# Layer 2 attention: odd score steps of the first round in spare PSUM banks, and the next layer's first work dealt anew over the last batch

## The chip, the core and the metric

The kernel runs on one core of a Trainium2 chip. It is one launch that computes a whole model of four layers, each an attention and a feed-forward block. The metric is the device time of one execution in microseconds. The engines are TensorE (PE, its weight loads PEld), VectorE (DVE), ScalarE (ACT), GpSimd (POOL) and SyncE (SP), which issues the DMAs. Each runs its own instructions in their order and waits on semaphores for the others.

## The reference, cut to what matters

The change lies in the attention of layer 2 and in the first steps of the local attention behind it. In the code, batches are `b` = 0 to 7, there are 256 queries and 512 keys, 16 heads of 64 elements, and everything is float32.

```python
def _L2_xattn_ref(x, context, mask, Wq, Wkv, Wout, b_out):
    q = x @ Wq.T                                   # x is layer-normed
    k, v = jnp.split(context @ Wkv.T, 2, axis=-1)
    ...                                            # to heads
    sim = jnp.einsum('bhid,bhjd->bhij', q, k) * SCALE
    sim = jnp.where(mask[:, None, None, :], sim, max_neg)
    attn = jax.nn.softmax(sim, axis=-1)
    out = jnp.einsum('bhij,bhjd->bhid', attn, v)
    return out.transpose(0, 2, 1, 3).reshape(B, Nq, HEADS * DIM_HEAD) @ Wout.T + b_out

# local attention (layer 2, feed-forward block), its first lines
h = shift_token(x)
q, k, v = jnp.split(h @ wqkv, 3, axis=-1)
q, k = l2norm(q) * qs, l2norm(k) * ksc
q, k = rotary_xpos(q, k)
```

## The kernel before, in words

`wide_attention` (L1645 to L2084) does the attention of layer 2. A batch is cut in two rounds of 8 steps (`s` = 0 to 7 and 8 to 15). A round takes 8 of the 16 heads, a step 32 queries of these heads. A step has two units (`w` = 0, 1) of 128x512 scores:

- PE, `scores` (L2019): 8 matmuls of 64x32 weights and 512 columns (two records each in the trace) into two PSUM banks, `s_ps0` and `s_ps1`. All steps use the same two banks, so a step waits until DVE has read both units of the step before (`max_ready`, L2025).
- DVE, `maxima` (L1812): one instruction per unit (L1820) adds the mask, negates, copies the scores to SBUF and takes the maximum.
- ACT, `exponentials` (L1942, L1949), then DVE, `turn_probs` (L1823, L1832): two 32x32-block transposes a step into `pT`.
- PE, `outputs` (L2034): the value products of a whole round (L2046) and the spread inverse sums (L2052) go into the four banks of `pv_ps`, a round late: in steps 3, 5 and 7 of the next round. In batch 0's first round there is no round before, and `pv_ps` lies idle. Behind the last round all 128 products come at once (L2069).

ACT copies half of `pv_ps` (`copy_inv`, L1959), DVE multiplies it into `o` (`normalise_outputs`, L1845) and, behind the last round, PE starts the next value products only then.

Every engine looks one step ahead: in step `s` PE issues the scores of `s + 1`, then the step's jobs. Jobs are projections (XT, Q, K, V, OUT) and, in the last batch, LOCAL 0 to 7: the shifted tokens (0), their transpose (1), queries and keys of two token tiles (2 to 5) and their values (6, 7). They are set by tables (L1664 to L1671), and each goes through one of two ring banks, in turn: PE fills it, ACT (for OUT: DVE) drains it. A fill waits for the drain two jobs earlier. The local work of DVE and POOL on these results is in `FirstLocal`: `copy_half` (L1605) and `tables` (L1594), `sum_squares` (L1608), `rotate` (L1615), `normalise` (L1627), `power` (L1589). Before, LOCAL 0 to 5 stand in steps 10 to 15 and LOCAL 6 and 7 behind the last value products. The block ends with the output of batch 7, its moments and scaling (L1915 to L1918); then all engines meet and the local attention starts.

Of the kernel before, what the change touches and what calls it, by code (L numbers as in the profile page):

```python
# [14 lines left out]
B = 8  # L15
# [3 lines left out]
TPB = S // P  # L19
# [5 lines left out]
BLK = 32  # L25
# [1619 lines left out]
def wide_attention(m):  # L1645
# [21 lines left out]
    next_batch = {7: [(XT, 0)], 9: [(K, 0), (K, 1)], 10: [(K, 2), (K, 3)], 12: [(Q, 0), (Q, 1)]}  # L1667
    last_batch = {13: [(OUT, 0)], 14: [(OUT, 1)]}
    end_values = {8: [(V, 2), (V, 3)], 9: [(V, 4), (V, 5)], 10: [(V, 6), (V, 7)]}
    for_local = {10: [0], 11: [1], 12: [2], 13: [3], 14: [4], 15: [5]}  # L1670
    blocks_of = {3: range(0, 5), 5: range(5, 10), 7: range(10, 16)}  # L1671

    def step_jobs(b, s):
# [8 lines left out]
        return jobs  # L1682
    before = [(XT, 0, 0), (Q, 0, 0), (Q, 0, 1)]
    steps = {(b, s): step_jobs(b, s) for b in range(B) for s in range(STEPS)}
    behind = [(LOCAL, B - 1, 6), (LOCAL, B - 1, 7), (OUT, B - 1, 0), (OUT, B - 1, 1)]
    jobs = before + [job for b in range(B) for s in range(STEPS) for job in steps[b, s]] + behind
    number = {job: n for n, job in enumerate(jobs)}

    with ExitStack() as ctx:
# [24 lines left out]
        s_ps = [psum(m, ctx, f"s_ps{n}_l2x", [P, KV]) for n in range(2)]  # L1714
        pv_ps = psum(m, ctx, "pv_ps_l2x", [P, NC, 512])

        bank = lambda job: ring[number[job] % RING]
        fills = lambda job: m.filled[number[job] % RING].sem
        drains = lambda job: m.drained[number[job] % RING].sem
# [12 lines left out]
        with nc.Block() as block:  # L1732
# [15 lines left out]
            @block.gpsimd  # L1748
            def _(pool):
                def power(t0, t1, n):  # L1750
                    pool.wait_ge(*m.var_eps.after(n))
                    pool.tensor_tensor(rs[:, t0:t1], ve[:, t0:t1], k["minus_half"][:, 0:t1 - t0], ALU.pow).then_inc(m.row_rstd.sem, 1)

                def add_bias(b):
                    pool.wait_ge(*m.normed.after(TPB * (b + 1)))
                    rows = x[:, TPB * b:TPB * (b + 1), :]
                    pool.tensor_tensor(rows, rows, bo[:].unsqueeze(1).to_broadcast([P, TPB, D]), ALU.add).then_inc(m.bias_added.sem, 1)

                def spread_inv(n):
                    pool.wait_ge(*m.sums_inverted.after(n + 1))  # L1760
                    if n >= ROUNDS:
                        pool.wait_ge(*m.pv_done.after(n - 1))
                    pool.tensor_tensor(spread[n % ROUNDS][:], inv[:].unsqueeze(2).to_broadcast([P, 2 * QB, BLK]),  # L1763
                                       k["eye32"].unsqueeze(1).to_broadcast([P, 2 * QB, BLK]), ALU.mult).then_inc(m.inv_spread.sem, 1)

                def out_power(b):
                    cols = slice(TPB * b, TPB * (b + 1))
                    pool.wait_ge(*m.out_eps.after(b + 1))
                    pool.tensor_tensor(out_rs[:, cols], out_ve[:, cols], k["minus_half"][:, 0:TPB], ALU.pow).then_inc(m.out_rstd.sem, 1)

                power(0, TPB, 1)
                power(TPB, NT, 2)
                pool.wait_ge(*m.bias_loaded.after(16))
                add_bias(0)
                add_bias(1)
                for n in range(LAST + 1):
                    if n >= 3 and n % 2 == 1:
                        out_power((n - 3) // 2)
                    if n == LAST:
                        local.power(pool, 0)  # L1780
                    spread_inv(n)
                    if n % 2 == 1 and n // 2 + 2 < B:
                        add_bias(n // 2 + 2)
                local.power(pool, 1)
                out_power(B - 1)

            @block.vector
            def _(dve):
# [23 lines left out]
                def maxima(b, s):  # L1812
                    if s == 0:
                        dve.wait_ge(*m.mask_ready.after(b + 1))
                    for w in range(2):
                        n = 2 * s + w
                        dve.wait_ge(*m.scores_ready.after(UNITS * b + n + 1))
                        if UNITS * b + n >= 4:
                            dve.wait_ge(*m.turned.after(UNITS * b + n - 3))
                        dve.tensor_tensor_reduce(out=probs[n % 4][:], in0=s_ps[w][:], in1=mask_b[b % 2][:], scale=-1.0, scalar=3e38,  # L1820
                                                 op0=ALU.add, op1=ALU.min, accum_out=nmax[:, b % 2, n:n + 1]).then_inc(m.max_ready.sem, 1)

                def turn_probs(b, s):  # L1823
# [57 lines left out]
                for b in range(B):  # L1881
                    for s in range(STEPS):
                        n = ROUNDS * b + s // QB
                        if ahead(b, s)[0] < B:
                            maxima(*ahead(b, s))
                        turn_probs(b, s)
                        if s % QB == 1 and n >= 2:
                            normalise_outputs(n - 2)
                        if s % QB == 0 and n >= 1:
                            invert_sums(n - 1)  # L1890
                        for job in steps[b, s]:
                            drain(job)
                        if s == 14 and b > 0:
                            out_moments(b - 1)
                        if s == 15 and b > 0:
                            out_scale(b - 1)
                        if s == 6 and b + 1 < B:
                            convert_mask(b + 1)
                        if s == 10 and b + 2 < B:
                            scale(b + 2)  # L1900
                        if b + 1 == B and s == 9:
                            dve.wait_ge(*m.out_normed.after(2 * TPB))
                            local.copy_half(dve)
                            local.tables(dve)
                        if b + 1 == B and s == 14:
                            local.sum_squares(dve, 0)
                normalise_outputs(LAST - 1)
                invert_sums(LAST)
                dve.wait_ge(*m.scores_ready.after(UNITS * B))
                local.rotate(dve, 0, empty_local)  # L1910
                local.sum_squares(dve, 1)
                local.rotate(dve, 1, empty_local)
                local.normalise(dve, 0)
                normalise_outputs(LAST)
                local.normalise(dve, 1)  # L1915
                for job in behind:
                    drain(job)
                out_moments(B - 1)  # L1918
# [3 lines left out]
            def _(act):  # L1922
# [48 lines left out]
                        if s % QB == 0 and n >= 2:  # L1971
                            copy_inv(n - 2)
                copy_inv(LAST - 1)
                for job in behind[0:TPB]:
                    drain(job)
                copy_inv(LAST)

            @block.tensor
            def _(pe):
# [39 lines left out]
                def scores(b, s):  # L2019
                    r, qb = divmod(s, QB)  # L2020
                    if qb == 0:
                        for of in of_scores(b, r):
                            pe.wait_ge(*empty(of))
                    if (b, s) > (0, 0):
                        pe.wait_ge(*m.max_ready.after(UNITS * b + 2 * s))  # L2025
                    for w in range(2):
                        rows = slice(hd * w, hd * (w + 1))
                        for c in range(NC):
                            g = NC * r + c
                            ins = pe.matmul(s_ps[w][BLK * c:BLK * (c + 1), :], q[rows, g, BLK * qb:BLK * (qb + 1)], kT[rows, g, :],  # L2030
                                            start=True, stop=True)
                        ins.then_inc(m.scores_ready.sem, 1)

# [1559 lines left out]
```

## Time and profile before

| what | us |
|---|---|
| median of 3 runs (1711.23, 1711.42, 1713.07) | 1711.42 |
| the profiled execution's own time | 1709.85 |
| its span, first to last instruction | 1707.8 |
| `wide_attention`, from its first DVE statistics to its last scaling | 476.75 to 959.64 |
| PE, DVE, ACT, POOL busy, of the span | 1494.0, 1300.6, 1029.0, 569.3 |

Times in rows are microseconds from the span's start. A busy PE is one with a matmul in flight; PEclk 1.00 is TensorE's higher clock level (2.4 GHz), 0.50 the lower (1.2 GHz). The two ends of `wide_attention` are where the change is: 484 to 514 is batch 0's first round and the steps behind it, 908 to 960 the end of batch 7.

### The profile page before, as it was taken

The numbers are of one execution on the slowest core, as the hardware profiler recorded it, in microseconds if no ns is written. First come the engines' busy times: TensorE is split into PE (matmuls) and PEld (weight loads), VectorE is DVE, ScalarE is ACT, GpSimd is POOL, SyncE is SP. The second block draws the span as 40 slices with busy tenths as digits, with TensorE's granted clock in tenths as the row PEclk, the third lists the DMA queues.
The fourth block names the chain that finished last, engine by engine and source line by source line (L and its number), as shares of the span: only waits on it lengthen the run. The fifth ranks groups of instructions, "written<-read, shape, count | busy, mean of one in ns | idle before, by whom it ended". The sixth has DMA issues, their size and how long they took to land. (4 is left out here: it accounts for less than half of the span.)

```text
span 1707.8 us, 45809 instructions
## 1 busy us (share of the span) xinstructions
PE 1494.0 (87%) x17532; PEld 805.7 (47%) x17532; DVE 1300.6 (76%) x3513; ACT 1029.0 (60%) x2227; POOL 569.3 (33%) x618
## 2 busy tenths in 40 slices
PE   5886999997658999999998799987899787999976
PEld 3631344343423555555555566654566552333333
DVE  5636688885968787878877799857899557898848
ACT  2230666665936566666665499843898532777764
POOL 0306565621010000000001599615899104243200
PEclk9885899998869999999999999998999985999997
DMA  5123443411010000000000000010100003222100
GB/s 172 31 35 103 113 82 89 80 33 44 9 40 2 3 9 9 9 9 3 29 2 3 7 1 0 1 49 8 42 0 0 15 6 81 50 48 44 31 2 25
DMA packets 61570, 56.41 MB, mean 33 GB/s; under 512 B 9866, under 2 KB 53054, under 8 KB 61254
## 3 DMA queue, kind: packets, MB, share of 16 engines
q1 hardware_dynamic: 60518, 53.42, 13.0%
q8 instruction: 129, 2.11, 0.5%
q14 instruction: 59, 0.48, 0.1%
q10 hardware_dynamic: 864, 0.39, 0.1%
HBM read 30.59 MB, written 1.05 MB: 19 GB/s over the span
## 5 line engine op out<-in xcount | busy, mean ns | idle before, releaser
L1949 ACT ACTIVATE probs_l2x<-probs_l2x,nmax_l2x 128x512 f32<-128x512 f32 x256 | 182.8, 715 | 161.0 <-DVE nmax_l2x L1820 160.9
L1820 DVE CUSTOM_DVE_ANT_0 probs_l2x<-s_ps_l2x,mask_b_l2x 128x512 f32<-128x512 f32 x256 | 166.3, 687 | 92.3 <-PE s_ps_l2x L2030 90.8
L1087 DVE CUSTOM_DVE_ANT_0 junk_l1x<-s_ps_l1x,mask_b_l1x 128x512 bf16<-128x512 f32 x256 | 166.2, 686 | 44.6 <-PE s_ps_l1x L1292 42.7
L1090 DVE TENSOR_REDUCE nmax_l3x<-s_ps_l3x 128x1 f32<-128x512 f32 x256 | 163.7, 683 | 32.3 <-PE s_ps_l3x L1292 30.5
L1149 ACT ACTIVATE pT_l1x<-st_ps_l1x 128x1024 f32<-128x1024 f32 x128 | 131.0, 1023 | 72.6 <-PE st_ps_l1x L1277 72.5
L1832 DVE STREAM_TRANSPOSE pT_l2x<-probs_l2x 128x512 f32<-128x512 f32 x256 | 166.3, 688 | 0.0
L2030 PE MATMUL s_ps_l2x<-kT_l2x_first,q_l2x 64*32 64x512 f32 x2048 | 144.7, 622 | 16.8 <-DVE nmax_l2x L1820 15.9
L2046 PE MATMUL pv_ps_l2x<-pT_l2x,v_l2x_first 32*64 32x256 f32 x4096 | 122.3, 379 | 2.5 <-issue 2.5
L2641 POOL TENSOR_TENSOR rn_l2a_first<-ssc_l2a_first,consts 128x16 f32<-128x16 f32 x28 | 109.1, 3896 | 20.2 <-DVE ssc_l2a_first L2668 20.0
L2811 ACT ACTIVATE probs_l2a<-minus_s_l2a,nmax_l2a 128x128 f32<-128x128 f32 (+1 forms) x256 | 106.1, 424 | 9.5 <-DVE nmax_l2a L2716 9.5
L2046 PEld LDWEIGHTS pv_ps_l2x<-pT_l2x,v_l2x_first 32*64 32x64 f32 x4096 | 90.0, 131 | 39.2 <-issue 15.3
L1763 POOL TENSOR_TENSOR spread_l2x<-inv_l2x,consts 128x512 f32<-128x512 f32 x16 | 17.6, 1100 | 270.1 <-DVE inv_l2x L1839 270.1
L2597 POOL TENSOR_TENSOR v_l2x_first<-kT_l2x_first,tb_l2a_first 128x256 f32<-128x256 f32 x112 | 103.9, 958 | 3.3 <-ACT kT_l2x_first L2779 2.7
L2716 DVE CUSTOM_DVE_ANT_0 minus_s_l2a<-s_ps_l2a,consts 128x128 f32<-128x128 f32 (+1 forms) x256 | 67.3, 317 | 30.5 <-PE s_ps_l2a L2929 26.3
L1292 PE MATMUL s_ps_l3x<-kT_l3x_first,q_l3x 51*128 51x512 bf16 x192 | 74.3, 428 | 15.2 <-DVE nmax_l3x L1090 8.4
L1304 PE MATMUL pv_ps_l1x<-pT_l1x,v_l1x 128*32 128x256 f32 x1024 | 82.5, 396 | 1.6 <-ACT o_l1x L1157 1.4
L1292 PE MATMUL s_ps_l1x<-kT_l1x_first,q_l1x 48*128 48x512 bf16 x192 | 72.3, 433 | 12.1 <-DMA q_l1x<-parts_l1x_first 8.0
L1149 ACT ACTIVATE v_l2x_first<-st_ps_l3x 128x1024 f32<-128x1024 f32 x64 | 65.2, 1024 | 23.8 <-PE st_ps_l3x L1277 23.8
L1149 ACT ACTIVATE kT_l2x_first<-st_ps_l3x 128x1024 f32<-128x1024 f32 x64 | 65.2, 1023 | 20.4 <-PE st_ps_l3x L1277 19.9
L1277 PE MATMUL st_ps_l3x<-q_l3x,kT_l3x_first 54*128 54x256 bf16 x384 | 64.7, 280 | 0.0
L1277 PE MATMUL st_ps_l1x<-q_l1x,kT_l1x_first 51*128 51x256 bf16 x384 | 62.5, 283 | 0.0
L2030 PEld LDWEIGHTS s_ps_l2x<-kT_l2x_first,q_l2x 64*32 64x32 f32 x2048 | 23.6, 106 | 79.5 <-DVE nmax_l2x L1820 45.9
(533 smaller groups left out, 3637.9 us busy)
## 6 DMA issues: line engine op xcount, KB each, us to landing
mask_i_l1x<-in_mask SPq DMA_DIRECT2D x8, 512.0 KB, 4.8
maskT_i_l1x<-in_mask_t SPq DMA_DIRECT2D x8, 512.0 KB, 5.3
kT_l1x_first<-parts_l1x_first SPq DMA_DIRECT2D x60, 64.0 KB
kT_l3x_first<-parts_l3x_first SPq DMA_DIRECT2D x60, 64.0 KB
q_l1x<-parts_l1x_first SPq DMA_DIRECT2D x90, 32.0 KB
q_l3x<-parts_l3x_first SPq DMA_DIRECT2D x90, 32.0 KB
ctxT_l0x<-in_ctxT SPq DMA_DIRECT2D x9, 256.0 KB, 3.2
rows_l0x<-in_ctx SPq DMA_DIRECT2D x9, 256.0 KB, 4.4
```

The lines of the kernel that those rows point to most:

```text
L1087: dve.tensor_tensor_reduce(out=junk[w][:], in0=s_ps[w][:], in1=mask_b[b % 2][:, j, :], scale=-1.0, scalar=3e38, op0=ALU.add, op1=ALU.min, ...
L1090: dve.tensor_reduce(to, s_ps[w][:], AX.X, ALU.max, negate=True).then_inc(m.s_drained[w].sem, 1)
L1149: act.activation(pT[t % 4][:, :, 2 * j:2 * j + 2, :].rearrange("p w c t -> p w (c t)"), st_ps[j][:], ACT.Exp)\
L1277: ins = pe.matmul(st_ps[j][:, w, e * S:(e + 1) * S], kT[b % NST][rows, p, c * P:(c + 1) * P], q[b % NST][rows, p, :], start=not masked, st ...
L1292: pe.matmul(s_ps[w][:], q[b % NST][rows, p, j * P:(j + 1) * P], kT[b % NST][rows, p, :], start=True, stop=True)\
L1820: dve.tensor_tensor_reduce(out=probs[n % 4][:], in0=s_ps[w][:], in1=mask_b[b % 2][:], scale=-1.0, scalar=3e38, op0=ALU.add, op1=ALU.min, a ...
L1832: dve.transpose(pT[r][:, w, :, BLK * qb:BLK * (qb + 1)], probs[unit % 4][:].rearrange("p (k t) -> p k t", t=BLK))\
L1949: act.activation(probs[n % 4][:], probs[n % 4][:], ACT.Exp, bias=nmax[:, b % 2, n:n + 1], scale=-1.0, accum_out=sums[:, r, w, qb:qb + 1]). ...
L2030: ins = pe.matmul(s_ps[w][BLK * c:BLK * (c + 1), :], q[rows, g, BLK * qb:BLK * (qb + 1)], kT[rows, g, :], start=True, stop=True)
L2046: pe.matmul(pv_ps[hd * w:hd * (w + 1), c, 0:S], v[BLK * c:BLK * (c + 1), r, kb, hd * w:hd * (w + 1)], pT[r][BLK * c:BLK * (c + 1), w, kb, ...
L2641: pool.tensor_tensor(rn[:, cols], ssc[:, cols], k["minus_half"][:, 0:2 * NH], ALU.pow).then_inc(m.powers_ready.sem, 1)
L2811: act.activation(probs[n % (2 * DEEP)][:, cols], minus_s[n % (2 * DEEP)][:, cols], ACT.Exp, bias=nmax[:, u, TPB * n + j:TPB * n + j + 1], ...
```

## The change

Two parts.

**Scores.** In batch 0, steps 1, 3, 5 and 7 write their scores to banks 0 and 1 of `pv_ps` instead of `s_ps`, and DVE reads them there. The wait before a step's scores names the last step that used the same banks: two steps back in steps 2 to 8, none in step 1.

**Local work.** LOCAL 0 to 7 move to steps 5, 7, 11, 12, 12, 13, 15, 15 of the last batch; nothing but the output is left behind the value products. On DVE, `copy_half` and `tables` move from step 9 to step 4, `sum_squares(0)` from 14 to 13, `sum_squares(1)` and `rotate(0)` from behind the round to step 15 (ahead of `normalise_outputs(LAST - 1)`), and both `normalise` go ahead of `normalise_outputs(LAST)`. POOL does both powers before it spreads the last inverse sums.

```diff
-    for_local = {10: [0], 11: [1], 12: [2], 13: [3], 14: [4], 15: [5]}
+    for_local = {5: [0], 7: [1], 11: [2], 12: [3, 4], 13: [5], 15: [6, 7]}
...
-    behind = [(LOCAL, B - 1, 6), (LOCAL, B - 1, 7), (OUT, B - 1, 0), (OUT, B - 1, 1)]
+    behind = [(OUT, B - 1, 0), (OUT, B - 1, 1)]
...
+        spare = lambda b, s: b == 0 and s < QB and s % 2 == 1
+        score_bank = lambda b, s, w: pv_ps[:, w, :] if spare(b, s) else s_ps[w][:]
+        last_user = lambda b, s: s - 2 if b == 0 and 2 <= s <= QB else s - 1
...
                     if n == LAST:
                         local.power(pool, 0)
+                        local.power(pool, 1)
                     spread_inv(n)
...
-                local.power(pool, 1)
...
-                        if b + 1 == B and s == 9:
+                        if b + 1 == B and s == 4:
                             dve.wait_ge(*m.out_normed.after(2 * TPB))
                             local.copy_half(dve)
                             local.tables(dve)
-                        if b + 1 == B and s == 14:
+                        if b + 1 == B and s == 13:
                             local.sum_squares(dve, 0)
+                        if b + 1 == B and s == 15:
+                            local.sum_squares(dve, 1)
+                            dve.wait_ge(*m.scores_ready.after(UNITS * B))
+                            local.rotate(dve, 0, empty_local)
                 normalise_outputs(LAST - 1)
                 invert_sums(LAST)
-                dve.wait_ge(*m.scores_ready.after(UNITS * B))
-                local.rotate(dve, 0, empty_local)
-                local.sum_squares(dve, 1)
                 local.rotate(dve, 1, empty_local)
                 local.normalise(dve, 0)
+                local.normalise(dve, 1)
                 normalise_outputs(LAST)
-                local.normalise(dve, 1)
...
-                for job in behind[0:TPB]:
-                    drain(job)
...
-                    if (b, s) > (0, 0):
-                        pe.wait_ge(*m.max_ready.after(UNITS * b + 2 * s))
+                    if b > 0 or s > 1:
+                        pe.wait_ge(*m.max_ready.after(UNITS * b + 2 * (last_user(b, s) + 1)))
```

On PE the start of batch 0 reads as follows before, from the scores of step 0 on (`x7` stands for the other seven matmuls of a step):

```order
L2030 MATMUL s_ps_l2x<-kT_l2x_first,q_l2x 32x512 [waits bank0_drained,bank1_drained]
L2030 MATMUL s_ps_l2x<-kT_l2x_first,q_l2x 32x512 x7
L2030 MATMUL s_ps_l2x<-kT_l2x_first,q_l2x 32x512 [waits max_ready]
L2030 MATMUL s_ps_l2x<-kT_l2x_first,q_l2x 32x512 x7
L2030 MATMUL s_ps_l2x<-kT_l2x_first,q_l2x 32x512 [waits max_ready]
L2030 MATMUL s_ps_l2x<-kT_l2x_first,q_l2x 32x512 x7
```

and after the change:

```order
L2032 MATMUL s_ps_l2x<-kT_l2x_first,q_l2x 32x512 [waits bank0_drained,bank1_drained]
L2032 MATMUL s_ps_l2x<-kT_l2x_first,q_l2x 32x512 x7
L2032 MATMUL pv_ps_l2x<-kT_l2x_first,q_l2x 32x512 x8
L2032 MATMUL s_ps_l2x<-kT_l2x_first,q_l2x 32x512 [waits max_ready]
L2032 MATMUL s_ps_l2x<-kT_l2x_first,q_l2x 32x512 x7
L2032 MATMUL pv_ps_l2x<-kT_l2x_first,q_l2x 32x512 [waits max_ready]
L2032 MATMUL pv_ps_l2x<-kT_l2x_first,q_l2x 32x512 x7
```

Step 1 follows step 0 with no wait, and from step 2 on the wait named is for the maxima of two steps before.

On DVE the end of batch 7, from the last transposes on, reads before (`o_l2x<-pv_ps_l2x` is `normalise_outputs`; the rows on `kT_l2x_first`, `scratch_l2x` and `wq_l2x_first` are rotations and sums of squares):

```order
L1611 TENSOR_REDUCE ss_l2a_first<-scratch_l2x 128x16 [waits local_squared]
L1613 TENSOR_SCALAR ssc_l2a_first<-ss_l2a_first 128x16 [waits local_summed]
L1832 STREAM_TRANSPOSE pT_l2x<-probs_l2x 128x16x32 [waits probs_ready] x2
L1870 TENSOR_SCALAR y_l2a_first<-x_tok,out_mv_l2x,out_rs_l2x 128x128 [waits out_rstd]
L1870 TENSOR_SCALAR y_l2a_first<-x_tok,out_mv_l2x,out_rs_l2x 128x128
L1845 TENSOR_TENSOR o_l2x<-pv_ps_l2x,o_l2x 128x1024 [waits inv_copied]
L1839 RECIPROCAL inv_l2x<-sums_l2x 128x16 [waits inv_spread,probs_ready]
L1619 TENSOR_TENSOR kT_l2x_first<-kT_l2x_first,ta_l2a_first 128x1024 [waits bank0_drained,local_tables,scores_ready]
```

and after the change:

```order
L1835 STREAM_TRANSPOSE pT_l2x<-probs_l2x 128x16x32 [waits probs_ready] x2
L1873 TENSOR_SCALAR y_l2a_first<-x_tok,out_mv_l2x,out_rs_l2x 128x128 [waits out_rstd]
L1873 TENSOR_SCALAR y_l2a_first<-x_tok,out_mv_l2x,out_rs_l2x 128x128
L1611 TENSOR_REDUCE ss_l2a_first<-wq_l2x_first 128x16 [waits local_squared]
L1613 TENSOR_SCALAR ssc_l2a_first<-ss_l2a_first 128x16 [waits local_summed]
L1619 TENSOR_TENSOR kT_l2x_first<-kT_l2x_first,ta_l2a_first 128x1024 [waits bank1_drained,local_tables,scores_ready]
L1624 TENSOR_TENSOR scratch_l2x<-kT_l2x_first,tb_l2a_first 128x8x32 x4
L1848 TENSOR_TENSOR o_l2x<-pv_ps_l2x,o_l2x 128x1024 [waits inv_copied]
```

One pair of squares has left the place ahead of the transposes; the other pair and a rotation of five instructions now stand ahead of `normalise_outputs(LAST - 1)`.

## Rows read from the trace of the kernel before

**Rows 1.** Windows: engine, busy time, instructions; then PEclk, DMA share, GB/s.

```profile
484.00:514.00 30.00, 18.01 (x171) 4.31 (x170) 21.91 (x55) 15.23 (x40) 3.52 (x3) 0.72 0.00 2
514.00:930.00 416.00, 405.37 (x8119) 222.04 (x8112) 331.11 (x821) 263.83 (x639) 24.07 (x27) 1.00 0.03 8
```

**Rows 2.** Waits, 484 to 514: total us, times, longest.

```profile
PE s_ps_l2x L2030 <- DVE nmax_l2x L1820: 11.2, 8, 1.5
```

**Rows 3.** Timeline, steps 0 to 2 of batch 0: start, duration, engine, what.

```profile
484.81 1.09 PE L2030 MATMUL s_ps_l2x<-kT_l2x_first,q_l2x 64*32 64x512 f32 x16 [0.78 <-ACT q_l2x L1931]
...
487.27 0.60 DVE L1803 TENSOR_SCALAR xn_l2x<-x_tok,mv_l2x,rs_l2x 128x128 f32<-128x128 f32 x2
...
487.41 1.96 PE L2030 MATMUL s_ps_l2x<-kT_l2x_first,q_l2x 64*32 64x512 f32 x16 [1.50 <-DVE nmax_l2x L1820]
...
489.41 0.69 DVE L1820 CUSTOM_DVE_ANT_0 probs_l2x<-s_ps_l2x,mask_b_l2x 128x512 f32<-128x512 f32 x1 [1.53 <-PE s_ps_l2x L2030]
...
490.63 1.30 DVE L1832 STREAM_TRANSPOSE pT_l2x<-probs_l2x 128x512 f32<-128x512 f32 x2
...
492.77 0.69 DVE L1820 CUSTOM_DVE_ANT_0 probs_l2x<-s_ps_l2x,mask_b_l2x 128x512 f32<-128x512 f32 x1 [0.84 <-PE s_ps_l2x L2030]
```

**Rows 4.** Timeline, queries filled in step 4, maxima of steps 7 and 8.

```profile
502.76 2.73 PE L2009 MATMUL ring_l2x<-xnT_l2x,wq_l2x_first 128*128 128x256 f32 x8
...
509.05 0.69 DVE L1820 CUSTOM_DVE_ANT_0 probs_l2x<-s_ps_l2x,mask_b_l2x 128x512 f32<-128x512 f32 x1
...
511.80 0.68 DVE L1820 CUSTOM_DVE_ANT_0 probs_l2x<-s_ps_l2x,mask_b_l2x 128x512 f32<-128x512 f32 x1
```

**Rows 5.** Windows around PE's idle gaps, columns as in rows 1.

```profile
490.00:500.00 10.00, 5.89 (x48) 0.69 (x48) 7.48 (x19) 4.56 (x12) 0.00 (x0) 0.50 0.00 0
...
506.00:516.00 10.00, 4.50 (x74) 0.97 (x66) 9.45 (x24) 5.92 (x17) 0.00 (x0) 1.00 0.00 0
...
915.00:917.00 2.00, 2.00 (x20) 0.71 (x4) 0.84 (x3) 0.10 (x1) 0.00 (x0) 0.50 0.00 0
...
938.00:940.00 2.00, 1.08 (x40) 1.10 (x48) 2.00 (x4) 0.00 (x0) 0.95 (x1) 1.00 0.00 0
```

**Rows 6.** Timeline, PE in batch 7: LOCAL 0, next scores, next value products, LOCAL 6 and 7.

```profile
913.24 0.67 PE L1560 MATMUL ring_l2x<-y_l2a_first,consts 128*128 128x256 f32 x2 [2.44 <-ACT v_l2x_first L1935]
...
914.17 1.96 PE L2030 MATMUL s_ps_l2x<-kT_l2x_first,q_l2x 64*32 64x512 f32 x16
...
917.10 2.47 PE L2046 MATMUL pv_ps_l2x<-pT_l2x,v_l2x_first 32*64 32x256 f32 x80
...
946.45 1.98 PE L1572 MATMUL ring_l2x<-wqkv_l2a_first,hT_l2a_first 128*128 128x512 f32 x4
```

**Rows 7.** Timeline, last maxima to last output product.

```profile
929.34 0.69 DVE L1820 CUSTOM_DVE_ANT_0 probs_l2x<-s_ps_l2x,mask_b_l2x 128x512 f32<-128x512 f32 x1 [3.51 <-PE s_ps_l2x L2030]
...
935.76 0.57 DVE L1870 TENSOR_SCALAR y_l2a_first<-x_tok,out_mv_l2x,out_rs_l2x 128x128 f32<-128x128 f32 x2
...
937.59 1.23 DVE L1845 TENSOR_TENSOR o_l2x<-pv_ps_l2x,o_l2x 128x1024 f32<-128x1024 f32 x1 [1.26 <-ACT o_l2x L1959]
...
938.92 7.17 PE L2046 MATMUL pv_ps_l2x<-pT_l2x,v_l2x_first 32*64 32x256 f32 x256 [2.49 <-issue]
939.97 2.27 DVE L1624 TENSOR_TENSOR scratch_l2x<-kT_l2x_first,tb_l2a_first 128x256 f32<-128x256 f32 x4
942.16 1.21 DVE L1611 TENSOR_REDUCE ss_l2a_first<-wq_l2x_first 128x16 f32<-128x1024 f32 x1
...
943.65 3.81 POOL L1592 TENSOR_TENSOR rn_l2a_first<-ssc_l2a_first,consts 128x16 f32<-128x16 f32 x1 [2.70 <-DVE ssc_l2a_first L1613]
...
944.62 1.45 DVE L1624 TENSOR_TENSOR wq_l2x_first<-kT_l2x_first,tb_l2a_first 128x256 f32<-128x256 f32 x4
...
948.96 1.02 ACT L1959 ACTIVATE o_l2x<-pv_ps_l2x 128x1024 f32<-128x1024 f32 x1
...
951.29 5.47 PE L2016 MATMUL ring_l2x<-wo_l2x,o_l2x 128*128 128x128 f32 x32 [2.86 <-DVE o_l2x L1845]
```

More of the change, by code:

```diff
@@ L1819, in maxima @@
                             dve.wait_ge(*m.turned.after(UNITS * b + n - 3))
-                        dve.tensor_tensor_reduce(out=probs[n % 4][:], in0=s_ps[w][:], in1=mask_b[b % 2][:], scale=-1.0, scalar=3e38,
+                        dve.tensor_tensor_reduce(out=probs[n % 4][:], in0=score_bank(b, s, w), in1=mask_b[b % 2][:], scale=-1.0, scalar=3e38,
                                                  op0=ALU.add, op1=ALU.min, accum_out=nmax[:, b % 2, n:n + 1]).then_inc(m.max_ready.sem, 1)
@@ L2029, in scores @@
                             g = NC * r + c
-                            ins = pe.matmul(s_ps[w][BLK * c:BLK * (c + 1), :], q[rows, g, BLK * qb:BLK * (qb + 1)], kT[rows, g, :],
+                            ins = pe.matmul(score_bank(b, s, w)[BLK * c:BLK * (c + 1), :], q[rows, g, BLK * qb:BLK * (qb + 1)], kT[rows, g, :],
                                             start=True, stop=True)
```

## The prediction

> **What bounds the kernel now.** I read the windows first, to learn which engine fills each stretch. From 514 to 930 PE is busy 405 of 416 us at the full clock [rows 1]: there the order of PE's work sets the pace, and whatever is won ahead of this stretch is kept, as no fixed date lies in it. From 484 to 514 PE is busy only 18 of 30 us, at a mean clock of 0.72, and DVE 22 of 30 [rows 1]: nothing is full, so a chain bounds it. The list of waits names the chain: PE waits for maxima, eight times, 11.2 us [rows 2]. The timeline shows one turn of it: scores 1.96 us (487.41 to 489.37), two maxima (489.41 to about 490.7), and only then the next scores, because both steps use the same banks. The turn takes 492.77 - 489.41 = 3.36 us, of which DVE works 490.63 - 489.41 = 1.22 on maxima and 1.30 on transposes, 2.5 together [rows 3]. These scores run at the lower clock level (0.50 from 490 to 500 [rows 5]); at the higher one they take 1.09 [rows 3], and then the chain, 1.09 + 1.3 + gaps, is also 2.5: from step 7 on DVE stands with no idle time before it [rows 4]. So double banks can win only where the clock is low. Last I read the end of batch 7, where waits stand again: PE waits 2.44 us for a ring bank and then runs scores in 1.96 again [rows 6], and 2.49 before the last value products [rows 7].
>
> **First round, the scores.** Step 1's scores no longer wait; they follow step 0's (484.81 + 1.09) and are done by about 487, while DVE is busy until 487.27 + 0.60 = 487.87 [rows 3]. So the maxima of step 1 start at 487.87 instead of 489.41. From there DVE sets the turn, 2.5 us if scores come in time, and at half clock they do: 1.96 in a turn of 2.5. Step 7's maxima start at 487.87 + 6 x 2.5 = 502.9; before, 509.05 [rows 4]: 6.2 us earlier. One step can be late: behind step 5's scores stand two query fills, 2.73 us partly at half clock [rows 4]. Step 5's scores may start when step 3's maxima end (492.87 + 1.3 = 494.2), end at 496.2, the fills (2.7 to, at half clock throughout, 3.7) at 498.9 to 499.9, step 6's scores (1.1 to 2.0) at 500.0 to 501.9, and DVE wants them at 500.4: late by 0 to 1.5. I take 0.6, in the middle, since the denser PE work may raise the clock. The term is **-5.6** (bounds -4.7 and -6.2). PE writes one pair of banks while DVE reads the other, as it does now with value products beside maxima; I take 0.69 a maximum as it is.
>
> **Hand-off to the second round, a new gap.** Step 8's scores wait only for step 6 and are issued early; step 9's use the same banks as step 8's and wait for its maxima, at 511.80 - 5.6 + 1.3 = 507.5 [rows 4]. PE has finished step 8's scores and a transpose by about 503.5: idle some 4 us, where before no gap here was over 1.5 [rows 2]. This idle time costs nothing by itself, but the clock may fall: behind 2.44 us idle it was at 0.50 [rows 5, 6], behind 2.49 at 938 it stayed at 1.00 [rows 5, 7]. The low stretch after the former lasted from 913.24 to 917.10, 3.9 us [rows 6]. The same here costs at least nothing, where DVE covers it, and at most half of 3.9, 2.0, when the key fills (two of 128x512 in 1.98, by the same product in rows 6) make PE the bound. One turn of 3.36 for 2.5 is 0.9; I take **+1.0**.
>
> The Trainium skill, "TensorE: Matmul & The Clock Gate", section "Part 1: The HAM clock gate (the "warmup" mystery)", says that the throttled state is the default and activity releases it; its section "HAM oscillation" tells of a kernel which falls back at every long wait. By that rule alone both new gaps, this and the one at the end, would be followed by a low stretch, which is what my sum has; by the row at 938 one or both would not be.
>
> **Batch 7, up to its last scores.** LOCAL 0 leaves the place where it waited 2.44 us for ACT's drains [rows 6]; in step 5 only its own ring wait is left. But LOCAL 4 and 5 move ahead of the last scores, 1.98 us by the same two products [rows 6]. That is 0.4 won, less small ring waits where fills stand closer: 0 to 0.4, I take 0.1. With the gap goes the low stretch behind it: 3.9 us at half clock do 1.95 us of work, so 1.9 comes back, if no other gap over 2 us arises here, and I find none. Together **-2.0** (bounds 0 and -2.3). DVE's copy and tables in step 4 (seven instructions of at most 128x256, of which four take 1.45 [rows 7], so under 2.6) fall in its waits for scores, one of which was 3.51 [rows 7].
>
> **The end.** Call the start of the last maxima M (929.34 before [rows 7]). Before: y scaled by M + 7.0 (936.33), pv normalised from M + 8.25, last value products from M + 9.6, output products from M + 21.95. After: the first squares (1.21, with their small companion 1.3) have left, so y is scaled by M + 5.7. Then come the second squares, 1.3, and a rotation: 1.1 (943.5 to 944.62) and four smaller ones in 1.45 to 2.27, in all 2.6 to 3.4 [rows 7]. Normalising starts at M + 9.6 to 10.4 and takes 1.23; the last value products start at M + 10.9 to 11.7, **1.3 to 2.1 later**, and PE's gap of 2.49 grows to 3.8 to 4.6. They and the sums take 946.45 - 938.92 = 7.5 [rows 6, 7], to M + 18.4 to 19.2. Before, ACT's copy then came at 948.96, 2.5 after the products, because LOCAL 6 and 7 were filled and drained first [rows 6, 7]; now it follows at once. Copy 1.02, multiply 1.23 and hand-overs 0.2: output products at M + 20.9 to 21.7, 0.3 to 1.1 earlier; I take 0.7. What DVE does meanwhile (rotation 2.6, four of 128x1024 at 1.23 as in rows 7) is 7.5 us, ends with the products and is covered by the copy; if it were a microsecond longer it would show. POOL's second power (3.81) starts by M + 8, is wanted at about M + 15, and the spread of the inverse behind it at M + 18. Against this stands the clock: a gap of about 4 us, a low stretch of 3.9 within 7.5 us of matmuls, +1.9. The output products run at the low level already before (5.47 for 32), so nothing is added there. Together **+1.2** (bounds -1.1 and +1.6).
>
> **Sum.** -5.6 + 1.0 - 2.0 + 1.2 = -5.4. The profiled execution took 1709.85, so 1704.45. The three runs have a median of 1711.42, 1.57 more than that execution; the same difference taken, the forecast is 1711.42 - 5.4 = 1706.0. With all bounds good, -6.2 + 0 - 2.3 - 1.1 = -9.6 (1701.8); with all bad, -4.7 + 2.0 + 0 + 1.6 = -1.1 (1710.3).
>
> **Rivals.**
> - The clock stays high in both new gaps. For it: the gap at 936.4, and 44% busy PE at 1.00 between 506 and 516 [rows 5]. Against: both gaps are longer than the one that was followed by 0.50. -5.6 - 2.0 - 0.7 = -8.3: 1703.1.
> - The gain is mostly used up: step 6 late by the full 1.5, PE the bound in the whole low stretch of the hand-off, a low stretch again somewhere in batch 7 before its last scores, and rotation and clock both at their dear end: the sum above, -1.1, 1710.3. For it: each price has a row; against: they are independent, and the gap at 911 surely closes.
> - Slower: the low clock does not last 3.9 us behind the hand-off but runs on into the second round of batch 0. The 30 us from 484 show it can: 490 to 500 is all low, with PE 59% busy [rows 5]. Every microsecond of it in PE-bound steps costs 0.5, so it decides from 11 us more than I count; 16 more cost 8: 1711.4 - 5.4 + 8 = 1714. Against: there the chain kept PE idle every turn, while from step 9 on fills, scores and value products follow closely.
> - The banks free nothing, because something else held the scores. Rows 2 and 3 name only maxima; I give it no chance of its own.
>
> **How the numbers follow.** Forecast case 0.61, clock high in both 0.20, used up 0.13, low clock persisting 0.04, anything else 0.02. A measurement of this kernel tells 0.2%, 3.4 us, from no change, so 1708.0 is the border. The forecast and the high clock lie below it but for their dear edge (0.80 faster), used up lies within (0.15 with that edge), the rest is slower (0.05). The range 1702.4 to 1709.2 leaves out one in ten on either side.
>
> **What would show it.** In the profile after: maxima of step 1 at 487.9, turns of 2.5 until step 5, step 7 near 503.4; PE idle about 4 us before step 9's scores and a clock of 0.50 behind it; PE near 1.00 through batch 7 without the 2.44 gap; a gap of 3.8 to 4.6 before the last value products, the low clock in them, ACT's copy right behind. I am wrong if the turns stay over 3 us, if the first round's lead is gone before batch 1, or if the end from M to the last scaling (30.3 before) is longer than 32.5.

## The result, and the profile after

The changed kernel took 1700.35 us (median of 6 executions, 1697.82 to 1704.45) against 1711.43 for the kernel before (6, 1711.08 to 1713.70; three of them are those of the table above): ratio 0.9935, interval 0.992 to 0.995, or 11.1 us less. The forecast was 1706.0, the range 1702.4 to 1709.2. The direction was right, the gain was twice the forecast, and the time lies below the range.

The profiled execution took 1697.82 us, its span is 1695.8. Windows of the first round with the steps behind it, and of the rest up to the last maxima (columns as in [rows 1]):

```profile
479.00:509.00 30.00, 20.70 (x189) 6.08 (x190) 26.17 (x68) 17.67 (x47) 3.84 (x4) 0.73 0.00 1
509.00:919.00 410.00, 403.32 (x8091) 220.91 (x8091) 326.95 (x808) 262.77 (x634) 23.04 (x26) 1.00 0.03 8
```

Over the same 30 us from the first scores DVE now works 26.2 us where it worked 21.9 [rows 1]. The timeline (against [rows 3, 4]) of the first turns, of step 7's and 8's maxima, and of step 9's scores:

```profile
479.18 1.96 PE L2032 MATMUL s_ps_l2x<-kT_l2x_first,q_l2x 64*32 64x512 f32 x16 [0.78 <-ACT q_l2x L1935]
480.86 1.97 PE L2032 MATMUL pv_ps_l2x<-kT_l2x_first,q_l2x 64*32 64x512 f32 x16
...
485.47 0.65 DVE L1823 CUSTOM_DVE_ANT_0 probs_l2x<-s_ps_l2x,mask_b_l2x 128x512 f32<-128x512 f32 x1
...
487.89 0.65 DVE L1823 CUSTOM_DVE_ANT_0 probs_l2x<-pv_ps_l2x,mask_b_l2x 128x512 f32<-128x512 f32 x1
...
497.56 0.65 DVE L1823 CUSTOM_DVE_ANT_0 probs_l2x<-pv_ps_l2x,mask_b_l2x 128x512 f32<-128x512 f32 x1
...
500.29 0.68 DVE L1823 CUSTOM_DVE_ANT_0 probs_l2x<-s_ps_l2x,mask_b_l2x 128x512 f32<-128x512 f32 x1
...
501.64 1.96 PE L2032 MATMUL s_ps_l2x<-kT_l2x_first,q_l2x 64*32 64x512 f32 x16 [3.61 <-DVE nmax_l2x L1823]
...
506.90 3.50 PE L2013 MATMUL ring_l2x<-ctxT_l2x,wk_l2x_first 128*128 128x512 f32 x4
```

Step 1 follows step 0 at once, both at the lower clock (1.96 and 1.97 us); the turns are 487.89 - 485.47 = 2.42 us; step 7's first maxima start 497.56 - 479.18 = 18.4 us after the first scores, where it was 509.05 - 484.81 = 24.2 [rows 3, 4]. Then PE stands 3.61 us, and what follows runs at the lower clock: the scores of steps 9 and 10 in 1.96, the first two key fills in 3.50. In batch 7 the gap of 2.44 us [rows 6] is gone: LOCAL 0 has no idle time before it, and from 880 to 929, past the last scores, the clock stays at its higher level. LOCAL 0 in the timeline, and the window:

```profile
884.01 0.67 PE L1560 MATMUL ring_l2x<-y_l2a_first,consts 128*128 128x256 f32 x2
```

```profile
880.00:929.00 49.00, 45.62 (x964) 26.87 (x956) 39.05 (x97) 29.41 (x67) 7.23 (x4) 1.00 0.01 3
```

The end, against [rows 7] (the wait of 3.47 us is called "issue" by the profile, but DVE's multiplication, from 928.21, ends just before the products start):

```profile
918.96 0.69 DVE L1823 CUSTOM_DVE_ANT_0 probs_l2x<-s_ps_l2x,mask_b_l2x 128x512 f32<-128x512 f32 x1 [2.20 <-PE s_ps_l2x L2032]
...
923.87 0.56 DVE L1873 TENSOR_SCALAR y_l2a_first<-x_tok,out_mv_l2x,out_rs_l2x 128x128 f32<-128x128 f32 x2
...
925.70 1.23 DVE L1619 TENSOR_TENSOR kT_l2x_first<-kT_l2x_first,ta_l2a_first 128x1024 f32<-128x1024 f32 x1
926.84 1.44 DVE L1624 TENSOR_TENSOR scratch_l2x<-kT_l2x_first,tb_l2a_first 128x256 f32<-128x256 f32 x4
928.21 1.21 DVE L1848 TENSOR_TENSOR o_l2x<-pv_ps_l2x,o_l2x 128x1024 f32<-128x1024 f32 x1
...
929.52 8.85 PE L2048 MATMUL pv_ps_l2x<-pT_l2x,v_l2x_first 32*64 32x256 f32 x256 [3.47 <-issue]
...
938.90 1.02 ACT L1963 ACTIVATE o_l2x<-pv_ps_l2x 128x1024 f32<-128x1024 f32 x1 [11.72 <-PE pv_ps_l2x L2054]
...
941.24 3.84 PE L2018 MATMUL ring_l2x<-wo_l2x,o_l2x 128*128 128x128 f32 x32 [2.43 <-DVE o_l2x L1848]
```

The value products start 10.6 us after the last maxima (9.6 before) and take 8.85 instead of 7.17; the output products come 22.3 after them (21.95 before) but take 3.84 instead of 5.47.

Now each trace in four parts: ahead of the stage, its first batch, its middle and end, and what lies behind. "Stage" runs from the start of step 0's scores to the start of the last scaling; batch 1 is its first maxima. All times are in us. The first four rows are four profiled executions of the kernel before, the next three of the changed one; the rest are the experiments. PEclk is that of the first 200 us, in code that is the same in all of them.

| execution | PEclk 0 to 200 | start | to batch 1 | to last maxima | to last scaling | stage | behind |
|---|---|---|---|---|---|---|---|
| before, 1 | 0.81 | 484.81 | 50.19 | 394.33 | 29.97 | 474.5 | 748.5 |
| before, 2 (e5) | 0.85 | 478.06 | 50.20 | 394.42 | 29.97 | 474.6 | 750.2 |
| before, 3 (e10) | 0.81 | 485.69 | 50.12 | 394.48 | 29.92 | 474.5 | 750.4 |
| before, 4 (e11) | 0.85 | 479.55 | 53.48 | 392.92 | 31.66 | 478.1 | 752.3 |
| changed, 1 | 0.85 | 479.18 | 47.56 | 392.22 | 28.66 | 468.4 | 748.2 |
| changed, 2 (e6) | 0.85 | 480.56 | 46.60 | 392.23 | 28.66 | 467.5 | 748.9 |
| changed, 3 (e12) | 0.83 | 482.08 | 47.57 | 392.23 | 28.66 | 468.5 | 748.4 |
| e1 scores alone | 0.80 | 486.50 | 46.56 | 394.38 | 29.97 | 470.9 | 749.2 |
| e2 local alone | 0.85 | 481.89 | 50.22 | 392.18 | 28.65 | 471.1 | 749.1 |
| e3 power early | 0.86 | 476.50 | 50.21 | 394.41 | 32.71 | 477.3 | 752.1 |
| e4 power back | 0.85 | 479.16 | 47.55 | 392.18 | 28.63 | 468.4 | 749.4 |
| e7 step 9 too | 0.83 | 483.57 | 44.21 | 392.23 | 28.66 | 465.1 | 748.3 |
| e8 rotate behind | 0.84 | 482.02 | 47.89 | 392.24 | 26.00 | 466.1 | 750.3 |
| e9 both | 0.83 | 483.60 | 44.20 | 392.24 | 29.19 | 465.6 | 751.0 |

In the first pair of traces the stage is 6.0 us shorter, and 5.6 of the 12 us lie ahead of it, where nothing was changed. The experiments had to say why.

### The profile page after: what moved, and what is told of

The parts are those of the page before. It is cut to its first block and busy times, and to the rows that moved or that the text cites. A ratio compares the mean times of both kernels' runs of the same rounds, so it can differ in the third digit from the quotient of the medians.

```text
span 1695.8 us, 45799 instructions
## 1 busy us (share of the span) xinstructions
PE 1479.6 (87%) x17522; PEld 801.5 (47%) x17532; DVE 1301.7 (77%) x3513; ACT 1029.6 (61%) x2227; POOL 568.6 (34%) x618
## 5 line engine op out<-in xcount | busy, mean ns | idle before, releaser
L1823 DVE CUSTOM_DVE_ANT_0 probs_l2x<-s_ps_l2x,mask_b_l2x 128x512 f32<-128x512 f32 x248 | 161.1, 687 | 86.9 <-PE s_ps_l2x L2032 85.2
L2032 PE MATMUL s_ps_l2x<-kT_l2x_first,q_l2x 64*32 64x512 f32 x1984 | 137.7, 612 | 11.0 <-DVE nmax_l2x L1823 10.1
L2970 PE MATMUL t_ps_l2a<-consts,probs_l2a 128*128 128x128 f32 x384 | 56.6, 284 | 4.8 <-ACT probs_l2a L2813 4.4
```

The source lines that it names most:

```text
L1823: dve.tensor_tensor_reduce(out=probs[n % 4][:], in0=score_bank(b, s, w), in1=mask_b[b % 2][:], scale=-1.0, scalar=3e38, op0=ALU.add, op1=A ...
L2032: ins = pe.matmul(score_bank(b, s, w)[BLK * c:BLK * (c + 1), :], q[rows, g, BLK * qb:BLK * (qb + 1)], kT[rows, g, :], start=True, stop=True)
```

## The experiments

**e1 and e2: each part alone.** e1 has only `spare`, `score_bank` and `last_user`, e2 only the rest of the diff.

> The kernel before with the banks of the first round alone; the last batch as before. Inside wide_attention both theories expect the same: step 7's second maxima 5.9 us earlier after step 0's scores than before (24.24 us there), of which about 3.3 are given back at the hand-off, so 2.6 us ahead from batch 1 on. They differ in what lies ahead of it. Theory A (the part ahead of the stage, 5.7 us of the changed kernel's gain, is not made by the edit but by the phase in which TensorE's clock steps fall in unchanged code, and any change to the program can set it anew): the stage may start at 479 or at 485 us, and need not start where it does in the changed kernel: total 1703 or 1709. Theory B (the edit itself moves the early stages): a start at 479.2, total near 1703. Theory C (it is chance between executions): the start scatters from run to run and the median of the times is 1708.8, only the 2.6 below before.

> The kernel before with the local attention's first work dealt anew; all scores in the two old banks. Inside wide_attention: first round as before (24.24 us from step 0's scores to step 7's maxima), batch 7 up to the last maxima 2.05 us shorter, the end from the last maxima to the last scaling 29.0 instead of 30.3: together 3.4. Theory A (clock phase in unchanged code): start of the stage at 479 or 485 or elsewhere, total 1708.0 or 1702.3. Theory B (the edit): which of the two parts carries the 5.7 us must show, this one or the scores. Theory C (chance): median 1708.0.

e1: 1706.51 us (median of 12 executions; ratio to the kernel before 0.9975, interval 0.9961 to 0.9990). e2: 1707.57 (12; 0.9990, 0.9967 to 1.0013), not told from no change by its time. By the stage both do what was expected of them: e1 3.6 us to batch 1 (its first scores ran in 1.09 us and not in 1.96, which is the 0.9 over 2.6), e2 2.15 and 1.3. So the parts are independent within what the clock leaves open: 2.6 to 3.6 and 3.4 alone, 6.0 to 7.0 together. The starts, 486.50 and 481.89, are not that of the changed kernel: theory B has no part that carries the 5.7 us.

**e3 and e4: one POOL call moved**, in the kernel before (e3); e4 takes the same move back in the changed one.

```diff
                         local.power(pool, 0)
+                        local.power(pool, 1)
...
-                local.power(pool, 1)
```

> The kernel before with one POOL call moved: local.power(1) right behind local.power(0). The second squares come late here, so POOL's last spread waits for them; by the rows the power is wanted only at the very end, but the spread then starts about 4 us later than before, at M + 22, where the sums wait: inside the stage 0 to +3 us. Ahead of the stage nothing is touched at all. Theory A: the start of the stage moves off 484.8 (or off before's clock steps in the first 200 us) although nothing there is edited. Theories B and C: it stays at 484.8, within 0.5 us.

> The changed kernel with POOL's second power put back behind the spread of the last inverse sums. The power takes 3.1 us of the 6.2 ahead of the spread; spread and power are both done before the value products end, so inside the stage 0 (at most 0.5). Theory A: the start of the stage may leave 479.2 and the total may be anything from 1700 to 1706. Theories B and C: 1700.4, start at 479.2 (B) or scattered (C).

e3 took 1716.02 us (12), ratio 1.0033, interval 1.0015 to 1.0052: slower, by 2.6 to 8.9 us. Of this 2.7 us stand in the stage's end, as its trace shows; where the rest comes from, if it is more than scatter, no run shows.

```profile
934.58 3.81 POOL L1592 TENSOR_TENSOR rn_l2a_first<-ssc_l2a_first,consts 128x16 f32<-128x16 f32 x1 [5.19 <-DVE ssc_l2a_first L1613]
938.36 1.94 POOL L1763 TENSOR_TENSOR spread_l2x<-inv_l2x,consts 128x512 f32<-128x512 f32 x1
...
940.34 0.69 PE L2052 MATMUL pv_ps_l2x<-spread_l2x,consts 32*64 32x256 f32 x16 [2.49 <-POOL spread_l2x L1763]
```

The spread stands behind a power that waited 5.19 us for late squares, and PE waits 2.49 us for it; in the changed kernel, where the squares come in step 15, the same order costs nothing (e4: 1702.1, ratio 0.9953, interval 0.9934 to 0.9973; stage 468.4 as the changed one). And e3 starts the stage at 476.50, 8.3 us ahead of the first profile of before, with not one instruction changed ahead of it. That fells theory B, which had it at 484.8. (The expectation put theory C beside it there; as C was put for e1, a start that scatters, it allows 476.50.) Theory A, that any edit can set the early clock anew, is left by e3 and needs the next runs.

**e5, e10, e11: the kernel before again; e6, e12: the changed one again.** No edit.

> The changed kernel itself once more, beside many executions of the kernel before. Theory C (the stretches of low clock in unchanged code fall differently in every execution, whichever kernel): inside wide_attention the same as in the first profile to 0.1 us or so (step 7's maxima 18.38 after step 0's scores, batch 1 at 47.56, end 28.66 after the last maxima), while the start of the stage lies anywhere from 479 to 488 in prof time; the median over the executions then lies nearer to 1711 - 6 = 1704 than to 1700.35. Theory B (the edit moves the early stages): start at 479.2 again, median 1700.4.

> The kernel before once more, timed beside itself: the ratio must be 1.000, and the width of its interval says what such a comparison can tell. Theory C (the low clock ahead of wide_attention falls differently in each execution): the start of the stage leaves 484.8 by some us, either way, inside the stage all is as in the first profile (24.2 to step 7's maxima, 50.2 to batch 1, 394.3 to the last maxima, 30.0 to the end). Theory B (each kernel has its own fixed early stages): start at 484.8 within 0.5.

> As the last: another execution and another profile of the kernel before. Theory C: start between 476 and 487. What is open is whether the kernel before starts the stage late on the average (485) and the changed one early (479 to 480), which would explain a difference over 6 to 7 us, or both around 481.

> The kernel before, a fourth profile. The same question as in the last; theory C expects a scatter of the start of about 3 us (standard deviation) around 481, theory B 484.8.

> The changed kernel, a third profile, and a third comparison with the kernel before. Theory C: start anywhere between 476 and 487, inside the stage 46.6 to 47.6 to batch 1, 392.2, 28.7; ratio such that both medians differ by 6 to 7 us plus or minus 2. Theory B: start at 479 to 480 for the third time, median about 1701, ratio 0.9937.

The kernel before timed against itself (one set of 35 executions, against 12, 9 and 9 more) gave ratios of 0.9999, 1.0016 and 0.9996, with intervals about 0.0018 wide to either side: 3 us. The changed kernel gave 0.9937 (0.9924 to 0.9950) and 0.9958 (0.9942 to 0.9975). The starts of the kernel before, 484.81, 478.06, 485.69 and 479.55, scatter over 7.6 us with no edit at all, the last three on one chip. So theory C holds ahead of the stage, and no edit is needed to move the start, as theory A would have it. Whether an edit shifts the mean of the start by a microsecond or two, four and three profiles can't tell. In all fourteen profiles the start follows the clock of the first 200 us: 486.50 at 0.80, 484.81 and 485.69 at 0.81, 482 to 484 at 0.83 and 0.84, 478 to 482 at 0.85, 476.50 at 0.86. Going from 0.86 to 0.80 over 200 us is 24 us more at half clock, at most 12 us of work; 10.0 are seen. Between the first two profiles of the kernel before, the same instructions are 6.4 us apart by 185.5 us, of 6.75 at the start of the stage, and the distance grows where engines wait for matmuls. What makes the low stretches fall differently is not shown.

One forecast of theory C failed: for e6 it put the median nearer to 1704 than to 1700.35, and it was 1701.33 (6). In e12 the medians, 1703.10 and 1708.67, are 5.6 us apart, within its 6 to 7 plus or minus 2.

Theory C as I wrote it was also too simple inside the stage, which was to repeat to about 0.1 us. In e6 step 0's scores ran at the higher clock and batch 1 came 46.60 us after them, not 47.56. e11 is the kernel before and is 3.5 us longer there. PE at its hand-off and at its end:

```profile
507.40 1.96 PE L2030 MATMUL s_ps_l2x<-kT_l2x_first,q_l2x 64*32 64x512 f32 x16 [1.20 <-DVE nmax_l2x L1820]
510.77 1.96 PE L2030 MATMUL s_ps_l2x<-kT_l2x_first,q_l2x 64*32 64x512 f32 x16 [1.40 <-DVE nmax_l2x L1820]
512.66 3.78 PE L2011 MATMUL ring_l2x<-ctxT_l2x,wk_l2x_first 128*128 128x512 f32 x4
...
911.35 0.67 PE L1560 MATMUL ring_l2x<-y_l2a_first,consts 128*128 128x256 f32 x2 [2.44 <-ACT v_l2x_first L1935]
...
912.17 1.09 PE L2030 MATMUL s_ps_l2x<-kT_l2x_first,q_l2x 64*32 64x512 f32 x16
...
935.53 8.85 PE L2046 MATMUL pv_ps_l2x<-pT_l2x,v_l2x_first 32*64 32x256 f32 x256 [2.49 <-issue]
```

With gaps no longer than in the first profile the low clock stands behind the first round, where it did not; it is absent behind the 2.44 us gap, where it was [rows 6]; and it covers the last value products, 8.85 instead of 7.17 [rows 7]. Idle times of 2.4 to 3.2 us are followed by either level, and those of 3.45 to 3.61 us by the low one in every trace. The idle time ahead of seven pieces of PE work, and the level that the work behind it met, counted over the fourteen traces:

| work | idle time, us | low clock in it | high clock all through |
|---|---|---|---|
| output products, in the changed order | 2.43 | 1 (e9) | 7 |
| LOCAL 0 with the scores behind it, in the old order | 2.44 | 5 | 1 (e11) |
| last value products | 2.49 | 2 (e9, e11) | 6 |
| output products, in the old order | 2.86 | 6 | 0 |
| first products of the local attention, behind the stage | 3.20 to 3.21 | 2 (e3, e11) | 12 |
| last value products, in the changed order | 3.45 to 3.48 | 6 | 0 |
| scores of step 9 | 3.61 | 6 | 0 |

The first turns of e11 show one more thing. Its scores of steps 1 and 2 ran at the higher clock, on the two old banks:

```profile
482.15 1.09 PE L2030 MATMUL s_ps_l2x<-kT_l2x_first,q_l2x 64*32 64x512 f32 x16 [1.50 <-DVE nmax_l2x L1820]
...
483.28 0.69 DVE L1820 CUSTOM_DVE_ANT_0 probs_l2x<-s_ps_l2x,mask_b_l2x 128x512 f32<-128x512 f32 x1 [0.67 <-PE s_ps_l2x L2030]
...
485.77 0.69 DVE L1820 CUSTOM_DVE_ANT_0 probs_l2x<-s_ps_l2x,mask_b_l2x 128x512 f32<-128x512 f32 x1
```

The turn is 485.77 - 483.28 = 2.49 us, against 2.42 with double banks: at the higher clock the spare banks win next to nothing, and what they win depends on where the low clock falls.

**e7: step 9's scores in the spare banks too.**

```diff
-        spare = lambda b, s: b == 0 and s < QB and s % 2 == 1
+        spare = lambda b, s: b == 0 and s < QB + 2 and s % 2 == 1
-        last_user = lambda b, s: s - 2 if b == 0 and 2 <= s <= QB else s - 1
+        last_user = lambda b, s: s - 2 if b == 0 and 2 <= s <= QB + 2 else s - 1
```

> The changed kernel, with step 9's scores in the spare banks as well, so that they too wait only for maxima two steps back. Theory H1 (the 3.3 us given back behind the first round are the idle 3.6 us before step 9's scores and the low clock behind it): step 9's maxima at 23.5 after step 0's scores instead of 24.46, step 12's at 32.0 (31 to 33) instead of 35.2, batch 1 at 44.4 instead of 47.56; total 3.2 us under the changed kernel. Theory H2 (they are given back because PE is full from step 9 on, so nothing ahead of it is kept): step 12 at 35 and batch 1 at 47.5 as now, total unchanged.

The hand-off in its trace, PE:

```profile
500.96 1.09 PE L2032 MATMUL s_ps_l2x<-kT_l2x_first,q_l2x 64*32 64x512 f32 x16 [0.81 <-DVE nmax_l2x L1823]
501.99 0.44 PE L2007 MATMUL ring_l2x<-consts,xn_l2x 128*128 128x128 f32 x2
503.29 1.09 PE L2032 MATMUL pv_ps_l2x<-kT_l2x_first,q_l2x 64*32 64x512 f32 x16 [0.87 <-DVE nmax_l2x L1823]
506.04 1.09 PE L2032 MATMUL s_ps_l2x<-kT_l2x_first,q_l2x 64*32 64x512 f32 x16 [1.65 <-DVE nmax_l2x L1823]
507.06 1.98 PE L2013 MATMUL ring_l2x<-ctxT_l2x,wk_l2x_first 128*128 128x512 f32 x4
```

No gap over 1.93 us is left there (in e9, with the same edit, neither), scores take 1.09 and the fills 1.98. Step 9's maxima come 23.55 us after the first scores (24.46), step 12's 31.87 (35.21), batch 1 44.21: 3.3 us won, H1 by its numbers. PE was not full there (H2 falls): idle time and low clock gave the lead back. The total was to be 3.2 us under the changed kernel. It is 1702.05 (6; ratio 0.9938, interval 0.9918 to 0.9958), no lower than that of the changed kernel beside it, 1701.33; six executions that lie 12 us apart do not show 3.

**e8 and e9: the end.** e9 is e7 and e8 together.

```diff
-                            dve.wait_ge(*m.scores_ready.after(UNITS * B))
-                            local.rotate(dve, 0, empty_local)
                 normalise_outputs(LAST - 1)
                 invert_sums(LAST)
+                dve.wait_ge(*m.scores_ready.after(UNITS * B))
+                local.rotate(dve, 0, empty_local)
...
-                local.normalise(dve, 1)
                 normalise_outputs(LAST)
+                local.normalise(dve, 1)
```

> The changed kernel with the first rotation put behind normalise_outputs(LAST - 1) and the second normalise behind normalise_outputs(LAST). ACT's copy ends 8.2 after the last maxima, so the last value products start at 9.55 instead of 10.56 behind an idle time of 2.5 instead of 3.47. Theory H1 (the idle time before them is what lets the clock fall): they take 7.2 instead of 8.85, ACT's copy comes 2.6 earlier; if no low stretch comes later the output products start 2.6 earlier, end 26.0 instead of 28.66; if it then falls in them (5.47 for 3.84), 27.6. Theory H2 (the low stretch comes whatever the length of the idle time): 8.85 again, all 1.0 earlier, end 27.6 with 8.85 in the value products.

> Both edits of the last two in one kernel: if they are independent, -3.2 in batch 0 and -1.0 to -2.6 at the end against the changed kernel: 4.2 to 5.8 us under it, the shortest of all. If the edits hit each other only by the clock, the stage times inside wide_attention are still those of the two runs to 0.3 us.

The last value and output products, in e8:

```profile
931.73 7.17 PE L2048 MATMUL pv_ps_l2x<-pT_l2x,v_l2x_first 32*64 32x256 f32 x256 [2.49 <-issue]
...
941.75 3.84 PE L2018 MATMUL ring_l2x<-wo_l2x,o_l2x 128*128 128x128 f32 x32 [2.43 <-DVE o_l2x L1848]
```

and in e9, with the same instructions in the same order behind the same idle times (e9 differs from e8 only in step 9's scores of batch 0, 430 us earlier):

```profile
929.62 8.85 PE L2048 MATMUL pv_ps_l2x<-pT_l2x,v_l2x_first 32*64 32x256 f32 x256 [2.49 <-issue]
...
941.34 5.35 PE L2018 MATMUL ring_l2x<-wo_l2x,o_l2x 128*128 128x128 f32 x32 [2.43 <-DVE o_l2x L1848]
```

In e8 the end is 26.00 us as H1 said, in e9 it is 29.19, half a microsecond over the changed kernel. The edit wins 1.0 us by its order; the other 1.7 of e8, and the 3.2 between e8 and e9, are the clock's. H2, which had a low stretch whatever the gap, falls by e8. H1, that 2.5 us of idle time instead of 3.47 keeps the clock high, falls as a rule by e9: at this length the gap alone does not decide it. Medians: 1703.41 (0.9954, 0.9939 to 0.9970) and 1701.81 (0.9937, 0.9923 to 0.9951). e9 was to be the shortest of all, 4.2 to 5.8 us under the changed kernel; by the stage it is 2.8 under, and e7 is the shortest, 465.1; no median here shows any of the three better than the changed kernel.

## Why the prediction was wrong

**The step that failed** is the last of the sum: "the same difference taken, the forecast is 1711.42 - 5.4", and the range added up from the terms of the stage alone. It takes everything outside the stage as fixed. It is not: its start scatters over 10 us in the fourteen profiles and what lies behind it over 4; so does the total, with the kernel before itself spread from 1702.89 to 1718.81 in its 35 executions beside e5. Of the first pair's 12.0 us the stage has 6.0, what is ahead 5.6, what is behind 0.3. In the means of four and three profiles the stage goes from 475.4 to 468.1 (-7.3, e11 included), its start from 482.0 to 480.6 (-1.4) and what is behind from 750.3 to 748.5 (-1.8). Over all executions timed, the kernel before has a mean of 1710.5 (115, standard deviation 3.4) and the changed one 1701.7 (24, 2.4): 8.7 less, plus or minus 1.1 if all are taken as one sample. By the means of the three sets in which both were timed, on more than one chip, it is 11.1, 10.7 and 7.7. So 6 to 7 of the 11.1 us are the stage's, 2 to 3 are scatter of a comparison of six with six, and 1 to 3 us of the mean I cannot place: the profiles are too few to tell whether they are chance.

**The mechanism** was right in which waits go and which gaps come, and wrong in two prices of the clock. Inside the stage -5.4 was forecast and -6.0 measured between the first profiles. That they lie so close is luck: the hand-off cost 2.2 us more than forecast, and the end was 2.5 better.
- First round: -5.6 forecast, -5.9 to step 7's maxima. The turns are 2.42 (2.5 said), and step 6 was not late (0.6 said). Against this step 1's maxima came 3.84 us after the first scores and not 3.06, since step 0's scores ran at the lower clock; in e6 and e1, where they did not, the lead is 6.7.
- Hand-off: the gap of about 4 us came (3.61), the low clock too, but the price was 3.3 and not 1.0. I had let the clock return after 3.9 us; it was low through scores 9 and 10 and most of the key fills. The idle time cost nothing by itself, as said: step 9's maxima come 3.36 us behind step 8's, 0.9 over the 2.49 of before, and that is what its scores lost to the clock, 1.96 for 1.09. What failed is the price of one turn: against e7, step 9 lost 0.9, step 10 0.8, and step 11, behind the slow key fills, 2.0, of which 0.4 came back in step 12. Together that is the 3.3.
- Batch 7: -2.0 forecast, -2.1 measured. In e11 the gap of 2.44 had no low clock behind it, and there this term would be 0.7.
- The end: +1.2 forecast, -1.3 measured. Products at M + 10.6 (10.9 to 11.7 said), at 8.85 for 7.2 (1.7 of the 1.9 said), ACT's copy right behind; missed is that the output products got the high clock, 3.84 for 5.47. I had written "so nothing is added there" and not seen that something could be taken away. Their idle time is 2.43 where it was 2.86 (the table above).
- No rival on the clock came as put: at the hand-off it fell, at the end the low stretch moved from one product to another. High clock in both places came only with other edits (e7, e8). That it runs on for longer than its gap suggests, the slower rival, e11 shows in the kernel before: it can hit either side of a comparison. (The 44% busy in the first rival is 45% by its row, which changes nothing.)

A kernel on whose path the clock moves has a distribution of times, and the 3.4 us of the prediction was no bound of it: single executions of the kernel before lie 16 us apart. The first six lay closer than the rest, with a standard deviation of 1.1 us against 3.4 of all 115, so the interval of the result is likely too narrow as well. The Trainium skill, "TensorE: Matmul & The Clock Gate", section "Part 1: The HAM clock gate (the "warmup" mystery)", says that the hardware watches activity in a window that runs freely, not counted from the kernel's instructions. By that rule, the same gap may or may not be followed by the low level, and e8 against e9 agrees: 7.17 and 8.85 us for the same products behind the same 2.49. By the rule that I weighed, each gap a low stretch, both would be 8.85; for the gaps of 3.45 us and more it held every time, so both new gaps of the changed kernel cost the low clock in every profile. The window itself no run here shows.

## What to carry to other kernels

Before a sum is set against a median, look at how the same code's start of the changed stage varies between executions; a change is then read from stage times in repeated profiles, and the total only from many executions. Where a double buffer ends, the first step that goes back to single banks gets the whole lead as one idle gap: carry the spare banks on to a step that has other PE work beside it. A POOL call is free only as long as what it waits for is early: the same move cost 2.7 us of stage time in one kernel and nothing in the other. And a buffer that hides slow matmuls is worth only what the low clock would have cost: ask first at which level the turn was measured.

## What the runs showed of the hardware

- Behind 2.4 to 3.2 us of idle time TensorE ran at either clock level: 2.44 us in batch 7 was followed by the low one in three profiles of the kernel before and not in the fourth; 2.49 before the last value products by the high level in three and the low one in the fourth. Behind 3.45 to 3.61 us in the stage the low one came in all 12 cases.
- The same early code took from 476.5 to 486.5 us, in step with a mean granted clock of 0.86 to 0.80 over its first 200 us. The kernel before, on one chip, had single times from 1702.89 to 1718.81.
- Two 128x512 key fills took 1.98 us at the high level and 3.38 to 3.78 where the low one covered most or nearly all of them.
